# Macaron block on one core: the feed-forward pipeline restaged (first product and count in one slot, second product in one piece) and the row-maximum mask moved

## The chip, the core and the metric

One core of a Trainium2 chip (trn2). The metric is the device time in microseconds of one execution, median of the runs shown. One profiled execution gives the trace that is read below. Engines are called TensorE (PE; its weight loads PEld), VectorE (DVE), ScalarE (ACT), GpSimd (POOL) and SyncE (SP, here only a DMA queue).

## What is computed

Activations `x` of 2 sequences x 1024 tokens x 512. `LN` is a layer normalization without weights.

```
x = x + 0.5 * ffn(LN(x));  x = x + attention(LN(x));  x = x + 0.5 * ffn(LN(x))

ffn(x):       z = x @ ternary(W_syn).T + b_syn            # 512 -> 2048
              thresh = 204th largest of z in the row
              h = where(z >= thresh, relu(z), 0)
              out = h @ ternary(W_out).T + b_out          # 2048 -> 512
              return layernorm(x + out) * gamma + beta
ternary(W):   s = mean|W|;  clip(round(W / s), -1, 1) * s

attention(x): 16 heads of 32, low-rank keys, queries and values; causal softmax; output projection
```

## The kernel before

**Feed-forward.** The 2048 tokens are 16 tiles of 128 rows. Both feed-forwards (f = 0, 1) run the same software pipeline over slots s = -1 to 25. In each slot every engine works through its own list of stages, written out by hand in order; `do(stage, f, s, off)` runs the stage on tile s - off, if that tile exists. Semaphores alone couple the engines. The stages of one tile, with their offsets:

- `stats1`, `normal` (VectorE) and `rstd1` (POOL) at -1: the normalized tile `xn`. `x_turn` (TensorE, four f32 transposes into bank `xP`) at 0, split into an f16 high half `x_hi` (ScalarE) and low half `x_lo` (VectorE).
- `mm1` at 1, in quarters c = 0 to 3 of 512 columns: 8 matmuls of 128x512 for high and low half (line 473) and a bias row (line 478), into `zP`. `evac` (ScalarE, line 709) copies quarters 0 to 2 to `Z` at offset 1, quarter 3 at the head of the next slot (offset 2).
- `count` (ScalarE, line 738) at 2 to 6: five passes of an interpolating search for the threshold, each counting the elements above a trial value in a row of 2048. At the head of a slot `update` (VectorE, lines 1106 to 1127) waits for all counts of the slot before and computes the next trial values of all five tiles; each count waits for it. The updates run in slots 3 (`FIRST_UPD`) to 22 (`LAST_UPD`).
- `S_SEL` = 7: `below` (VectorE, line 1135) masks the tile, `pick` (lines 1141 to 1148) takes the top eight of what is left and the threshold among them and sets a flag per row; `ok_rows` (TensorE, line 519) sums the flags into `xP`; `keep_top` (VectorE) copies the sum to `oki` (line 1206), loads it into a register, branches (`If`, line 1208, an exact search that does not run on this data) and applies the threshold (line 1210). This signals `h_set`.
- `S_OUT` = 8: `h_turn` c (TensorE, line 493) transposes quarter c of the kept tile into one of the two banks of `hP`; from the third on it waits for the low half two quarters back. `h_hi` (ScalarE, line 719) and `h_lo` (VectorE, line 1095) split it; `mm2` c (TensorE, line 506; the last one with a bias row, line 510) multiplies it into `oP`. Quarters 0 and 1 of `mm2` are issued in slot 8 of the tile, 2 and 3 in slot 9, with `h_hi` and `h_lo` of quarter 3.
- `S_FIN` = 9: `residual` (VectorE, lines 1217 to 1221), `rstd2` (POOL), `normal2` (VectorE, line 1229). `final` (POOL, lines 900 to 903) one slot later; it waits for that slot's `below`.

TensorE's list in a slot, in short: `mm1` 0, `h_turn` 0, `x_turn`, `mm2` 2 | `mm1` 1, `h_turn` 1, `mm2` 3 | `mm1` 2, `ok_rows`, `h_turn` 2, `mm2` 0 | `mm1` 3, `h_turn` 3, `mm2` 1. "Full" slots are those with both a first and a second product; the slots ahead of them (the fill) have no second product, the slots behind (the drain) no first product. In the second feed-forward `out_proj` of the attention's second sequence (line 644) stands at the end of slots -1 to 5.

**Attention.** For each sequence and each group of four heads, two units of 512 queries. `core_order` makes one list of events that all engines follow. A "row" event is a score block (line 582) with, on the diagonal, a second matmul that adds the causal mask (line 585); VectorE takes its maximum per query (line 1312). Three banks (`rowP`) take turns. Later "col" events compute the same scores transposed with the maximum folded in (lines 603, 607), ScalarE takes the exponential (line 793), and "mix" events multiply with the values and with ones (line 619).

SP's queue loads the weights, then the attention weights once the last transpose of the first feed-forward is done (line 399).

## Time and profile before

| | |
|---|---|
| median of 3 runs | 1291.21 us (1290.18 to 1293.3) |
| the profiled execution | 1289.8 us, span 1288.0 us |
| mean granted clock of TensorE | 0.939 of 2.4 GHz |
| TensorE busy | 1110.0 us, 86% |
| VectorE busy | 916.6 us, 71% |
| ScalarE busy | 795.9 us, 62% |
| POOL busy | 297.3 us, 23% |
| first feed-forward, attention, second | to 386, to 928, to 1288 us |

Busy shares are averages over stretches with different limits. Where the text says "start to start", it is the distance between the starts of neighbouring instructions on one engine; the printed duration includes a tail that overlaps the next one. A timeline row gives start, duration, engine, line, operation, output and input, and how many instructions are merged (x8); behind it, in brackets, how long the engine was idle ahead of it, and what it waited for.

### The profile page before, as it was taken

What the parts mean: (1) busy time and instruction counts of PE and PEld (TensorE: products, weight loads), DVE (VectorE), ACT (ScalarE), POOL (GpSimd) and SP (SyncE); (2) the same over time, 40 slices, a digit from 0 to 9 for tenths busy, and PEclk for the clock granted to TensorE, in tenths of its full rate; (3) what the DMA queues carried; (4) which work ended last, traced back from release to release, by engine and by line L of the source; (5) the groups of instructions that cost most, each with busy time, mean ns of one, the idle gap of its engine ahead of it and who ended that gap; (6) DMA issues with size and microseconds to landing.
All of it is one profiled execution on the core that took longest, in us unless ns stands there. A gap on an engine that the chain in (4) does not pass through costs nothing.

```text
span 1288.0 us, 17909 instructions
## 1 busy us (share of the span) xinstructions
PE 1110.0 (86%) x6149; PEld 510.9 (40%) x6198; DVE 916.6 (71%) x2010; ACT 795.9 (62%) x1147; POOL 297.3 (23%) x379
## 2 busy tenths in 40 slices
PE   0896999987768789999999799999799799998776
PEld 0342555543334333333344333332244355554333
DVE  5766899889963787875334887782223699999995
ACT  5399888896213536657614356567248998888521
POOL 2100122222252143100220450002100013222224
PEclk9997999998887989999999899999899899999787
DMA  9200000000010122110000311110000000000000
GB/s 370 72 1 1 1 1 2 1 1 1 1 33 21 50 58 50 47 38 2 1 21 8 78 47 46 31 34 2 1 1 1 1 9 10 17 18 18 17 18 33
DMA packets 22284, 37.44 MB, mean 29 GB/s; under 512 B 5398, under 2 KB 7833, under 8 KB 21532
## 3 DMA queue, kind: packets, MB, share of 16 engines
q1 hardware_dynamic: 21404, 34.54, 8.5%
q0 software_dynamic: 768, 1.57, 0.5%
q8 instruction: 50, 0.82, 0.3%
q14 instruction: 62, 0.51, 0.1%
HBM read 19.17 MB, written 4.21 MB: 18 GB/s over the span
## 4 chain that ended last, share of the span: by engine, by line
PE 62%; DVE 20%; issue 7%; ACT 5%; SPq 3%; POOL 1%; DMA 1%; another core or an unknown queue 1%; DVEq 0%; POOLq 0%; ACTq 0%
PE zP L473 13%; PE oP L506 11%; PE xP L619 5%; PE oP L619 5%; PE zP L603 4%; PE zP L544 4%; PE hP L582 3%; PE hP L493 3%; DVE mx L1312 3%; PE hP L644 2%; DVE arena L1095 2%; PE zP L644 2%; DVE arena L1135 2%; ACT arena L738 2%; DVE m L1143 2%
## 5 line engine op out<-in xcount | busy, mean ns | idle before, releaser
L738 ACT ACTIVATE arena<-arena,X 128x2048 int8<-128x2048 f32 x160 | 319.5, 2003 | 4.7 <-DVE X L1127 4.7
L793 ACT ACTIVATE arena<-zP,asc 128x512 f32<-128x512 f32 (+3 forms) x384 | 201.0, 581 | 115.5 <-PE zP L607 84.4
L506 PE MATMUL oP<-T,arena 128*128 128x512 f16 x1024 | 261.2, 402 | 3.0 <-DVE arena L1217 3.0
L473 PE MATMUL zP<-T,arena 128*128 128x512 f16 x1024 | 251.0, 390 | 6.0 <-ACT arena L709 5.1
L1312 DVE TENSOR_REDUCE mx<-hP 128x1 f32<-128x512 f32 (+3 forms) x256 | 135.8, 551 | 36.5 <-PE hP L585 25.0
L719 ACT ACTIVATE arena<-hP,sc 128x512 f16<-128x512 f32 x128 | 88.3, 690 | 106.8 <-PE hP L493 106.8
L473 PEld LDWEIGHTS zP<-T,arena 128*128 128x128 f16 x1024 | 102.3, 100 | 130.3 <-issue 14.6
L506 PEld LDWEIGHTS oP<-T,arena 128*128 128x128 f16 x1024 | 103.4, 102 | 112.1 <-issue 26.3
L709 ACT ACTIVATE arena<-zP,sc 128x512 f32<-128x512 f32 x128 | 87.3, 686 | 81.2 <-PE zP L478 54.8
L603 PE MATMUL zP<-arena 98*128 98x512 f16 (+3 forms) x384 | 110.2, 332 | 2.6 <-DMA arena<-arena 1.7
L1095 DVE SCALAR_TENSOR_TENSOR arena<-hP,sc,arena 128x512 f16<-128x512 f32 x128 | 95.6, 747 | 9.0 <-ACT arena L719 7.9
L1210 DVE SCALAR_TENSOR_TENSOR arena<-arena,sel 128x2048 f32<-128x2048 f32 x32 | 76.7, 2397 | 34.0 <-issue 22.6
L1330 DVE RECIPROCAL arena<-arena 128x128 f32<-128x128 f32 x64 | 57.0, 924 | 61.4 <-ACT arena L806 61.4
L582 PE MATMUL hP<-arena 96*128 96x512 f16 (+3 forms) x256 | 85.2, 349 | 13.3 <-DVE mx L1312 12.9
L900 POOL TENSOR_TENSOR x_sb<-x_sb,bet 128x512 f32<-128x512 f32 x32 | 40.6, 1267 | 222.1 <-DVE arena L1135 222.1
L493 PE MATMUL hP<-identf,arena 128*128 128x128 f32 x512 | 84.2, 290 | 2.7 <-DVE arena L1095 1.4
L619 PE MATMUL oP<-arena 128*32 128x512 f32 (+3 forms) x768 | 81.8, 498 | 3.8 <-ACT arena L806 3.8
L1312 DVE TENSOR_REDUCE mx<-zP 128x1 f32<-128x512 f32 (+3 forms) x128 | 69.8, 546 | 19.9 <-PE zP L585 11.6
L619 PE MATMUL xP<-arena,onesf 128*32 128x512 f32 (+3 forms) x768 | 81.8, 498 | 0.0
L947 POOL TENSOR_TENSOR arena<-arena 128x512 f32<-128x512 f32 x16 | 20.3, 1269 | 255.1 <-DVE arena L1330 255.1
L493 PEld LDWEIGHTS hP<-identf,arena 128*128 128x128 f32 x512 | 68.4, 155 | 25.4 <-issue 4.9
L1135 DVE SCALAR_TENSOR_TENSOR arena<-arena,FIN 128x2048 f32<-128x2048 f32 x32 | 75.0, 2344 | 0.0
(177 smaller groups left out, 1581.6 us busy)
## 6 DMA issues: line engine op xcount, KB each, us to landing
arena<-arena SPq DMA_DIRECT2D x168, 64.0 KB, 2.0
arena<-in_w_synT SPq DMA_DIRECT2D x4, 1024.0 KB, 8.3
arena<-in_w_outT SPq DMA_DIRECT2D x4, 1024.0 KB, 14.7
out_dram<-x_sb SPq DMA_DIRECT2D x16, 256.0 KB, 2.0
x_sb<-in_x SPq DMA_DIRECT2D x3, 1024.0 KB, 14.0
arena<-in_w_o SPq DMA_DIRECT2D x2, 1024.0 KB, 5.0
arena<-arena POOLq DMA_DIRECT2D x24, 64.0 KB, 1.9
arena<-in_b_syn SPq DMA_DIRECT2D x1, 1024.0 KB, 12.1
```

The source lines that it names most:

```text
L473: pe.matmul(zP[:, c * CW:(c + 1) * CW], part[:, g % 2, k, :], T1[:, k, c * CW:(c + 1) * CW], start=(n == 0 and k == 0), stop=False)
L493: mm = pe.transpose(hP[:, c % 2, k * P:(k + 1) * P], Z[:, g % ZR, n0:n0 + P], identf[:, :])
L506: mm = pe.matmul(oP[:, :], part[:, k, :], T2[:, k, :], start=(c == 0 and n == 0 and k == 0), stop=False)
L582: mm = pe.matmul(rowP[bank][:, 0:w], stack[0:3 * HD, 0, h, t * P:(t + 1) * P], stack[0:3 * HD, 1, h, 512 * c:512 * c + w], start=True, sto ...
L603: mm = pe.matmul(colP[m % 3][:, q0:512], stack[0:3 * HD + 2, 1, h, kb * P:(kb + 1) * P], stack[0:3 * HD + 2, 0, h, qc * 512 + q0:(qc + 1) ...
L619: mm = pe.matmul((mixP if kind == "mix_v" else sumP)[h * HD:(h + 1) * HD, q0:512], v, PT[:, m % 2, h, q0:512], start=(kb == 0), stop=last, ...
L719: act.activation(hThi[:, 4 * c:4 * c + 4, :].rearrange("p k t -> p (k t)"), hP[:, c % 2, :], ACT.Copy, scale=SH).then_inc(sm["hT_hi"], 1)
L738: act.activation(junk[:, counted[0] % 2, :], Z[:, g % ZR, :], ACT.Sign, bias=X[:, 2, k:k + 1], accum_out=S[:, k:k + 1]).then_inc(sm["cnt"], 1)
L793: act.activation(PT[:, m // 4 % 2, h, q0:512], colP[m % 3][:, q0:512], ACT.Exp, scale=asc[:, g, 10:11]).then_inc(sm["exp_done"], 1)
L1095: dve.scalar_tensor_tensor(hTlo[:, ks, :].rearrange("p k t -> p (k t)"), hP[:, c % 2, :], SH, hThi[:, ks, :].rearrange("p k t -> p (k t)") ...
L1135: dve.scalar_tensor_tensor(M[:, :], Z[:, g % ZR, :], TF, Z[:, g % ZR, :], ALU.is_le, ALU.mult)\
L1312: dve.tensor_reduce(mx[:, h, t, c:c + 1], rowP[bank][:, 0:w], AX.X, ALU.max)\
```

## The change

All offsets from the count on become one smaller (`S_CNT` = 1: the first count in the slot of the first product; `S_SEL` 6, `S_OUT` 7, `S_FIN` 8), so there is one slot fewer. Quarter 3 is evacuated and its halves are made in their own slot. TensorE's list becomes `h_turn` 0, `mm1` 0, `h_turn` 1, `mm1` 1, `x_turn`, `h_turn` 2, `mm1` 2, `h_turn` 3, `mm1` 3, and then the whole second product `mm2` 0 to 3, with `ok_rows` ahead of quarter 2. VectorE's and ScalarE's lists are put in a new order; `keep_top` is split, so that the flag is read (`read_flag`), the last low half follows, and then the branch. In the attention the mask matmul of the row blocks goes, and VectorE adds a mask tile (`causal`, bf16) while it takes the maximum, in one `tensor_tensor_reduce` whose elementwise result goes to a scratch tile.

```diff
--- before.py
+++ after.py
@@ -25,7 +25,8 @@
 TARGET = TOPK - 4.5
 SSTAR = 2 * TARGET - N
 BIG = 1e30
-S_SEL, S_OUT, S_FIN = 2 + NC, 3 + NC, 4 + NC
+S_CNT = 1
+S_SEL, S_OUT, S_FIN = S_CNT + NC, S_CNT + NC + 1, S_CNT + NC + 2
 ZR = 8
 XR = 11
 XSCALE = 256.0
@@ -218,7 +219,8 @@
         bcols = sb("bcols", [P, 14], F32)
         ident16 = sb("ident16", [P, P], F16)
         identm = sb("identm", [P, P], F16)
-        maskq = sb("maskq", [P, P], F16)
+        causal = sb("causal", [P, 512], BF16)
+        scored = sb("scored", [P, 2, 512], BF16)
         maskk = sb("maskk", [P, P], F16)
         mx = sb("mx", [P, HG, BT, 2], F32)
         mm_ = sb("mm_", [P, HG * 4], F32)
@@ -360,7 +362,7 @@
             if i is not None:
                 stage(f, i, *a)
 
-        FIRST_UPD, LAST_UPD = 3, NT + S_SEL - 1
+        FIRST_UPD, LAST_UPD = S_CNT + 1, NT + S_SEL - 1
 
         def updates(f, s):
 
@@ -578,12 +580,9 @@
                             pe.wait_ge(sm["masks"], 2)
                             pe.wait_ge(sm["a_xT"], (b + 1) * BT)
                         w = min(512, (t + 1) * P - 512 * c)
-                        own = c == t // 4
-                        mm = pe.matmul(rowP[bank][:, 0:w], stack[0:3 * HD, 0, h, t * P:(t + 1) * P],
-                                       stack[0:3 * HD, 1, h, 512 * c:512 * c + w], start=True, stop=not own)
-                        if own:
-                            mm = pe.matmul(rowP[bank][:, w - P:w], identm[:, :], maskq[:, :], start=False, stop=True)
-                        mm.then_inc(sm["row_ps"], 1)
+                        pe.matmul(rowP[bank][:, 0:w], stack[0:3 * HD, 0, h, t * P:(t + 1) * P],
+                                  stack[0:3 * HD, 1, h, 512 * c:512 * c + w], start=True, stop=True)\
+                            .then_inc(sm["row_ps"], 1)
                     elif kind == "turn":
                         pe.wait_ge(sm["m_set"], m + 1)
                         for t in range(4):
@@ -648,16 +647,14 @@
             for f in range(NF):
                 for s in slots:
                     for c in range(4):
+                        do(h_turn, f, s, S_OUT, c)
                         do(mm1, f, s, 1, c)
+                        if c == 1 and (f, s) != (0, 0):
+                            do(x_turn, f, s, 0)
+                    for c in range(4):
                         if c == 2:
                             do(ok_rows, f, s, S_SEL)
-                        do(h_turn, f, s, S_OUT, c)
-                        if c == 0 and (f, s) != (0, 0):
-                            do(x_turn, f, s, 0)
-                        if c < 2:
-                            do(mm2, f, s, S_OUT + 1, c + 2)
-                        else:
-                            do(mm2, f, s, S_OUT, c - 2)
+                        do(mm2, f, s, S_OUT, c)
                     for i in out_tiles(f, s):
                         out_proj(1, i)
                     if f == 0 and s == 0:
@@ -722,7 +719,7 @@
             counted = [0]
 
             def count(f, s, k):
-                i = at(s, 2 + k)
+                i = at(s, S_CNT + k)
                 if i is None:
                     return
                 g = f * NT + i
@@ -815,20 +812,20 @@
             for f in range(NF):
                 for s in slots:
 
-                    do(evac, f, s, 2, 3)
-                    do(h_hi, f, s, S_OUT + 1, 3)
+                    do(h_hi, f, s, S_OUT, 0)
                     do(evac, f, s, 1, 0)
-                    do(h_hi, f, s, S_OUT, 0)
+                    count(f, s, 4)
+                    do(h_hi, f, s, S_OUT, 1)
+                    do(evac, f, s, 1, 1)
                     if (f, s) != (0, 0):
                         do(x_hi, f, s, 0)
-                    count(f, s, 4)
                     count(f, s, 3)
-                    do(evac, f, s, 1, 1)
-                    do(h_hi, f, s, S_OUT, 1)
+                    do(h_hi, f, s, S_OUT, 2)
+                    do(evac, f, s, 1, 2)
+                    do(h_hi, f, s, S_OUT, 3)
+                    do(evac, f, s, 1, 3)
                     count(f, s, 2)
                     count(f, s, 1)
-                    do(evac, f, s, 1, 2)
-                    do(h_hi, f, s, S_OUT, 2)
                     count(f, s, 0)
                 if f == 0:
                     barrier(act, 1)
@@ -843,7 +840,7 @@
         def counts_before(f, s):
 
             per_f = NC * NT
-            return f * per_f + sum(1 for t in range(-1, s) for k in range(NC) if at(t, 2 + k) is not None)
+            return f * per_f + sum(1 for t in range(-1, s) for k in range(NC) if at(t, S_CNT + k) is not None)
 
         @block.gpsimd
         def _(pool):
@@ -866,11 +863,11 @@
             pool.wait_ge(sm["ident_set"], 2)
             link(pool.tensor_copy(ident16[:, :], identf[:, :]))
             link(pool.tensor_scalar(identm[:, :], identf[:, :], MASK, None, ALU.mult))
-            link(pool.memset(maskq[:, :], 0.0))
+            link(pool.memset(causal[:, :], 0.0))
             link(pool.memset(maskk[:, :], 0.0))
 
-            pool.affine_select(out=maskq[:, :], in_=maskq[:, :], compare_op=ALU.is_ge, fill=-MASK, base=0,
-                               pattern=[[-1, P]], channel_multiplier=1).then_inc(sm["masks"], 1)
+            pool.affine_select(out=causal[:, 384:512], in_=causal[:, 384:512], compare_op=ALU.is_ge, fill=-MASK * MASK,
+                               base=0, pattern=[[-1, P]], channel_multiplier=1).then_inc(sm["masks"], 1)
             pool.affine_select(out=maskk[:, :], in_=maskk[:, :], compare_op=ALU.is_ge, fill=-MASK, base=0,
                                pattern=[[1, P]], channel_multiplier=-1).then_inc(sm["masks"], 1)
             link(pool.memset(nhalf[:, :], -0.5))
@@ -1200,13 +1197,19 @@
                     step(dve.tensor_tensor(HIT, HIT, OPEN, ALU.mult))
                     add_found(HIT, BOUND)
 
-            def keep_top(f, i):
+            def read_flag(f, i):
                 g = f * NT + i
                 dve.wait_ge(sm["ok_sum"], g + 1)
                 dve.tensor_copy(oki[:, :], xP[:, 0:1]).then_inc(sm["ok_read"], 1)
+
+            def search_if_open(f, i):
+                g = f * NT + i
                 dve.wait_ge(sm["ok_read"], g + 1)
                 with dve.If(dve.value_load(oki[0:1, 0:1], min_val=0, max_val=P) < P):
                     search_down(Z[:, g % ZR, :])
+
+            def keep_top(f, i):
+                g = f * NT + i
                 dve.scalar_tensor_tensor(Z[:, g % ZR, :], Z[:, g % ZR, :], TH, Z[:, g % ZR, :], ALU.is_ge, ALU.mult)\
                     .then_inc(sm["h_set"], 1)
 
@@ -1309,8 +1312,15 @@
                         h, t, c = e[2:]
                         w = min(512, (t + 1) * P - 512 * c)
                         dve.wait_ge(sm["row_ps"], m + 1)
-                        dve.tensor_reduce(mx[:, h, t, c:c + 1], rowP[bank][:, 0:w], AX.X, ALU.max)\
-                            .then_inc(sm["row_max"], 1)
+                        if c == t // 4:
+                            if m >= 2:
+                                dve.wait_ge(sm["row_max"], m - 1)
+                            dve.tensor_tensor_reduce(scored[:, m % 2, 0:w], rowP[bank][:, 0:w], causal[:, 512 - w:512],
+                                                     1.0, -BIG, ALU.add, ALU.max, mx[:, h, t, c:c + 1])\
+                                .then_inc(sm["row_max"], 1)
+                        else:
+                            dve.tensor_reduce(mx[:, h, t, c:c + 1], rowP[bank][:, 0:w], AX.X, ALU.max)\
+                                .then_inc(sm["row_max"], 1)
                     elif kind == "max":
                         dve.wait_ge(sm["row_max"], n["row"])
                         link(dve.tensor_reduce(mm_[:, :], mx[:, :, 4 * e[2]:4 * e[2] + 4, :], AX.X, ALU.max))
@@ -1360,20 +1370,22 @@
                         ternary(1, s - 2)
                     if FIRST_UPD <= s <= LAST_UPD:
                         update(f, s)
-                    do(h_lo, f, s, S_OUT + 1, 3)
+                    do(h_lo, f, s, S_OUT, 0)
+                    do(residual, f, s, S_FIN)
                     do(below, f, s, S_SEL)
-                    do(h_lo, f, s, S_OUT, 0)
+                    do(h_lo, f, s, S_OUT, 1)
                     if (f, s) != (0, 0):
                         do(x_lo, f, s, 0)
                     if (f, s) == (0, 1):
                         search_start()
                     do(pick, f, s, S_SEL)
-                    do(h_lo, f, s, S_OUT, 1)
-                    do(residual, f, s, S_FIN)
+                    do(h_lo, f, s, S_OUT, 2)
                     if (f, s) != (0, -1):
                         do(stats1, f, s, -1)
+                    do(read_flag, f, s, S_SEL)
+                    do(h_lo, f, s, S_OUT, 3)
+                    do(search_if_open, f, s, S_SEL)
                     do(keep_top, f, s, S_SEL)
-                    do(h_lo, f, s, S_OUT, 2)
                     if (f, s) != (0, -1):
                         do(normal, f, s, -1)
                     if (f, s) == (0, 0):
@@ -1385,6 +1397,7 @@
                     barrier(dve, 1)
                     for i in range(BT):
                         normal_rows(0, i)
+                    dve.wait_ge(sm["masks"], 1)
                     link(dve.memset(mx[:, :, :, :], -BIG))
                     for b in range(2):
                         project(b)
```

## Rows read from the trace of the kernel before

**Rows 1.** Busy time by stretch: us; PE, PEld, DVE, ACT, POOL; clock; DMA.

```profile
189.19:206.44 17.25, 17.20 (x92) 9.29 (x92) 15.72 (x37) 15.12 (x21) 5.36 (x7) 1.00 0.00 1
304.00:319.60 15.60, 11.59 (x56) 5.82 (x55) 14.34 (x33) 9.10 (x12) 4.58 (x5) 0.89 0.00 1
466.00:637.00 171.00, 163.49 (x1348) 58.78 (x1348) 116.41 (x230) 108.77 (x209) 35.28 (x28) 0.98 0.12 32
```

**Rows 2.** The chain of waits in the first attention core, 466 to 637 us.

```profile
by line: PE xP L619 18.4%; PE oP L619 18.3%; PE zP L603 16.4%; PE hP L582 11.9%; DVE mx L1312 9.0%; PE zP L582 5.7%; PE zP L607 3.6%; DVE arena L1330 3.5%; issue 3.2%; ACT arena L793 2.2%; PE hP L585 2.0%; ACT arena L806 1.1%; PE hP L590 1.
```

**Rows 3.** Timeline of TensorE in a steady slot.

```profile
207.68 1.89 PE L473 MATMUL zP<-T,arena 128*128 128x512 f16 x8
...
209.41 0.38 PE L478 MATMUL zP<-brow,bones 128*128 128x512 bf16 x1
...
209.62 0.60 PE L493 MATMUL hP<-identf,arena 128*128 128x128 f32 x4
...
210.06 1.89 PE L506 MATMUL oP<-T,arena 128*128 128x512 f16 x8
```

**Rows 4.** Timeline of VectorE in a steady slot.

```profile
202.84 0.16 DVE L1106 TENSOR_SCALAR X<-S 128x5 f32<-128x5 f32 x1
...
205.21 2.34 DVE L1135 SCALAR_TENSOR_TENSOR arena<-arena,FIN 128x2048 f32<-128x2048 f32 x1
...
207.59 0.75 DVE L1095 SCALAR_TENSOR_TENSOR arena<-hP,sc,arena 128x512 f16<-128x512 f32 x1
...
208.86 0.15 DVE L1141 TENSOR_SCALAR sel<-FIN 128x1 f32<-128x1 f32 x1
...
212.18 0.75 DVE L1095 SCALAR_TENSOR_TENSOR arena<-hP,sc,arena 128x512 f16<-128x512 f32 x1 [0.23 <-ACT arena L719]
212.85 0.74 DVE L1217 SCALAR_TENSOR_TENSOR arena<-oP,sc,arena 128x512 f32<-128x512 f32 x1
...
214.45 0.66 DVE L1069 BATCH_NORM_STATS2 st<-x_sb 128x6 f32<-128x512 f32 x1
...
216.24 2.35 DVE L1210 SCALAR_TENSOR_TENSOR arena<-arena,sel 128x2048 f32<-128x2048 f32 x1 [0.87 <-DVE oki L1206]
```

**Rows 5.** Timeline of ScalarE in a steady slot.

```profile
208.90 2.01 ACT L738 ACTIVATE arena<-arena,X 128x2048 int8<-128x2048 f32 x1
...
210.89 0.69 ACT L709 ACTIVATE arena<-zP,sc 128x512 f32<-128x512 f32 x1
...
212.02 2.01 ACT L738 ACTIVATE arena<-arena,X 128x2048 int8<-128x2048 f32 x1
```

**Rows 6.** Timeline of VectorE: updates of both feed-forwards, the last residual of the first.

```profile
63.18 0.17 DVE L1106 TENSOR_SCALAR X<-S 128x5 f32<-128x5 f32 x1
...
117.37 0.17 DVE L1106 TENSOR_SCALAR X<-S 128x5 f32<-128x5 f32 x1 [0.35 <-ACT arena L738]
...
348.95 0.16 DVE L1106 TENSOR_SCALAR X<-S 128x5 f32<-128x5 f32 x1
...
378.81 0.75 DVE L1217 SCALAR_TENSOR_TENSOR arena<-oP,sc,arena 128x512 f32<-128x512 f32 x1 [3.83 <-PE oP L510]
...
978.95 0.16 DVE L1106 TENSOR_SCALAR X<-S 128x5 f32<-128x5 f32 x1
...
1017.24 0.17 DVE L1106 TENSOR_SCALAR X<-S 128x5 f32<-128x5 f32 x1 [0.31 <-ACT arena L738]
```

**Rows 7.** Timeline of TensorE in a drain slot, first burst behind the flag matmuls.

```profile
312.30 3.17 PE L506 MATMUL oP<-T,arena 128*128 128x512 f16 x8 [0.39 <-DVE arena L1217]
```

**Rows 8.** Timeline: a mask matmul and its successor; a row maximum; an accumulator read.

```profile
546.52 0.22 PE L585 MATMUL zP<-maskq,identm 128*128 128x128 f16 x1
...
546.58 0.38 PE L603 MATMUL zP<-arena 98*128 98x512 f16 x1
...
547.63 0.68 DVE L1312 TENSOR_REDUCE mx<-hP 128x1 f32<-128x512 f32 x1
...
209.19 0.08 DVE L1142 DVE_READ_ACCUMULATOR e<-ranks,sel 128x1 f32 x1
```

## The prediction

> **What bounds the kernel now.** I read the busy time by stretch first. In a steady slot of the feed-forward (17.25 us) TensorE is busy 17.20, VectorE 15.72, ScalarE 15.12, at full clock; in a slot of the drain (15.60 us, no first product left) TensorE has 11.59 and VectorE 14.34; in the first attention core TensorE has 163.5 of 171 us and VectorE 116.4 [rows 1]. The chain of waits inside the core is nearly all TensorE lines, with 9.0% for the row maxima on VectorE [rows 2]. So the change must be priced by stretch. The parts of a steady slot on TensorE, start to start, are: one quarter of a product with its bias row 1.94 us, without it 1.73, four transposes 0.44 [rows 3]. Five groups of transposes, four first-product quarters with bias, four second-product quarters and one bias row (0.21) make 17.1; with the flag matmuls this is the measured 17.25, without a gap.
>
> VectorE's parts, also start to start [rows 4]: a low half of the hidden tile 0.67 (212.18 to 212.85), so the update is 1.71 of the 2.37 from 202.84 to 205.21; `below` 2.38; `x_lo` 0.60 (the rest of 207.59 to 208.86); `pick` 3.1 (208.86 to 212.18, less the 0.23 of waiting printed there); residual with its statistics 1.60. The wait printed in front of `keep_top` begins at 215.37, so `stats1` and the flag's cast fill 0.92 from 214.45 (I split them 0.80 and 0.12), and from the cast to the start of `keep_top` it is 0.99; `keep_top` 2.27, its printed 2.35 less the 0.08 by which neighbours overlap. The slot's remainder to the next update (17.25 after 202.84) is a low half, `normal` and `normal2`, 0.46 each. On ScalarE a count is 1.99 and an evacuation plus a high half 1.13 [rows 5].
>
> **The fill gets shorter.** Each update waits for all counts of the slot before, and each count for its update: 1.83 on the way (1.71, and an estimated 0.12 to the count's start). Before, two evacuations and `x_hi` ran beside the update. After, the count of a tile comes in the slot of its evacuation, and only one evacuation covers the update: with five counts 1.83 + 9.95 + 3 x 0.57 + 0.49 (`x_hi`) + 0.17 (accumulator read; both estimated from their neighbours) = 14.2, where two evacuations less make it 13.1 before. With four counts 11.1 as before, with three 9.0, with two 8.44 (VectorE, which quantizes the second weights then). First feed-forward: the first update, at 63.18, comes one slot earlier, where that slot was 6.7 long without an update: 56.5. Five slots of 8.44, 9.0, 11.1, 14.2, 14.2 give 113.4 for what was at 117.37: 4.0 gained. Second feed-forward: the slots up to 978.95 are set by TensorE (out-projection); two of 14.2 follow, 1007.3 against 1017.24: 9.9 gained [rows 6]. Sum 13.9.
>
> **The full slot gets a VectorE loop.** TensorE's work is the same 17.25. But the order now closes a loop through both engines: update 1.71, low half 0.66, residual 1.60 (moved ahead), `below` 2.38, second low half 0.75 until its signal, then the fourth group of transposes (it needs that bank): 7.14. From there TensorE issues 0.44 + 1.94 + two quarters 3.46 = 5.84 until the flag matmuls, which take 0.40 to VectorE's cast (an estimate, somewhat under the 0.44 of four transposes); 0.99 + 0.07 of dispatch to `keep_top`, 2.27, `normal` and `normal2` 0.92. Sum 17.6 against 17.25. Here I chose that the register load of the `If` runs beside the low half now placed in front of it. Bounds: 17.25 (TensorE alone) and 18.2 (the load waits 0.6 for the low half; no row shows the pair). ScalarE's loop is 17.3 and POOL's three additions still start behind `below`: no cost while they stay under 17.6.
>
> **The drain loses the early second product.** Before, quarters 2 and 3 of the previous tile and quarter 0 stand between the transposes, and VectorE alone sets 15.6. After, quarter 0 waits behind the fourth transposes (7.14 after the update) and the flag matmuls wait behind quarters 0 and 1. With a first product in the slot this is filled; without one TensorE has only 1.75 us of transposes in its first 8 us. In the old drain slot, with 4.0 of 15.6 us idle and a granted clock of 0.89 [rows 1], eight matmuls behind the flag matmuls took 3.17 us [rows 7], against 1.89 in [rows 3]: part of the slot runs at 1.2 and not 2.4 GHz. The Trainium skill has the rule ("TensorE: Matmul & The Clock Gate", "Why this matters for your kernels": keep matmuls dense, an idle stretch drops the clock to half); by it a drain slot is the 17.7 worked out next, and without it the 15.3 of rival B. From rows: at 8.0 start 16 matmuls; all at half speed would be 6.8 us (0.43 each, twice the 0.216 of [rows 3]), all at full 3.46. I take 5.5, nearer to the half, since the burst in [rows 7] was at half for nearly its eight: flag matmuls at 13.5, cast 13.9, `keep_top` 14.95, next update 17.7. Bounds: 15.3 (full speed) and 19.2 (half all through, or the load waits as well).
>
> **From the sixth update to the last** (117.37 to 348.95 before, 231.6 [rows 6]; the same span of the second feed-forward is taken as equal): after, the first full slot 16.9 (no residual), seven of 17.6, two of 17.25 (no further input tile), 1.5 for a start at half clock (bounds 0 and 3), four drain slots of 17.7: 246.9. That is 15.3 lost, twice: 30.6.
>
> **The tail** (last update to the last residual, 348.95 to 378.81: 29.9): flag and `keep_top` 17.3; transposes, high and low half to 19.4; residual of the tile before and second low half to 21.7; fourth transposes, then four quarters in one piece, 7.1 warm plus 2.4 at half clock: residual at 31.8. Bounds 27.4 and 33.5. Twice 1.9: 3.8. What follows (statistics and additions) stays. SP's loads of the attention weights hang on the last transposes, which now lie further ahead of that residual; no cost.
>
> **The attention edit.** The causal mask matmul of the row maxima goes: 256 of 128 columns (4 heads, 8 tiles, 4 groups, 2 sequences), each 0.06 us from its start to the next matmul's [rows 8]: 14.6 us of TensorE. In a stream that is TensorE 95% busy I count three quarters: 11 off. VectorE's maximum becomes an addition of the mask with a maximum. No row has this operation. Lower bound: the 0.68 of a reduce of 512, nothing added. Above it: an accumulator read of 0.08 [rows 8], 256 x 0.08 = 20 us of VectorE; the furthest row is a two-input pass at half rate, taken as 0.3 us more, which would bring VectorE to about 155 of 171. I take 0.08, as with the other accumulating operations. The Trainium skill ("VectorE: DVE Perf Modes", "Two Vector instructions with no wait between them") has an operation that writes out its accumulator as two instructions; by that the read is due, and were it one instruction, the sum would be 3 lower. On the path lie the stretches before the first exponentials and the 9% of [rows 2]: 5 lost. Net 6 gained (bounds: 12 gained, 10 lost). The wait for the own result two operations back is always past. The wider mask costs POOL some 0.3 us early, hidden behind the weight loads.
>
> **Sum.** -13.9 + 30.6 + 3.8 - 6 = +14.5. The profiled execution took 1289.8 us (span 1288.0) and the median is 1291.2, so 1304.3 to 1305.7: 1305.
>
> **Rivals.**
> A (the forecast), chance 0.60: as above, 1305. It decides where TensorE waits for the fourth transposes.
> B, faster, 0.24: TensorE keeps full speed through the drain, because transposes suffice as work, or a second half-speed stretch falls outside the path. Drain slots are then 15.3, the tail 27.4: -13.9 + 2 x (237.3 - 231.6) - 5 - 6 = -13.5, so 1277. For it: one slot fewer in each feed-forward, and the flag's wait covered. Against: [rows 7]. It decides from drain slots under 16.4: 1.3 x 8 less is 10 of the 14.5.
> C, slower still, 0.11: the register load waits for the low half, 0.6 in each of some 30 slots: 1323. [Rows 4] show nothing running beside it.
> D, 0.05: the masked maximum is much dearer than a reduce, and VectorE bounds the core, 10 or more per sequence on top of the forecast's feed-forward: about 1330. Against: old VectorE slack of 55 us per core.
> That the new order does nothing (the loops and the one slot fewer cancel) sits between A and B.
>
> **Numbers.** 1305; range 1277 to 1322, which holds B's figure and nearly C. 0.3% (4 us) is about what a measurement of this kernel can tell from no change. A, C, D leave a little on the near side: faster 0.24, same 0.09, slower 0.67.
>
> **What would show it.** Updates 17.6 us apart in full slots and 17 to 18.5 in the drain; in the drain the fourth transposes released by VectorE's second low half, the first eight matmuls behind them near 3.4 us, the cast waiting for the flag matmuls; a fill slot of 14.2; mask matmuls gone and the core 2 to 4 us shorter. Drain slots near 15.3 with a granted clock near 1.0 would make the forecast wrong, as would an accumulator read that costs 0.2 and more.

## The result, and the profile after

The kernel after takes 1306.9 us (median of 4 runs, 1304.0 to 1308.6), the kernel before 1291.7 (1290.2 to 1293.3): the ratio is 1.0115, with a 95% interval of 1.0091 to 1.0139. The change makes the kernel slower by 15 us, as forecast (1305). The profiled execution of the kernel after is its slowest run, 1308.6 us; against the 1289.8 of the profiled one before that is 18.8 us, and it is these 18.8 us that the traces below divide.

The page of the kernel after: span, busy time, granted clock.

```profile
span 1306.7 us, 17955 instructions
PE 1107.1 (85%) x5942; PEld 494.3 (38%) x5942; DVE 916.1 (70%) x2266; ACT 796.6 (61%) x1147; POOL 301.1 (23%) x379
PEclk9898999997787979999999799999899899998888
```

Busy time by stretch of the kernel after, as in [rows 1]: a steady slot, a drain slot, the first attention core.

```profile
188.49:206.04 17.55, 17.44 (x93) 9.14 (x92) 15.75 (x39) 15.24 (x20) 5.33 (x7) 1.00 0.00 0
309.87:327.05 17.18, 11.48 (x53) 5.95 (x51) 14.35 (x33) 8.58 (x10) 4.55 (x5) 0.80 0.00 0
480.08:649.44 169.36, 161.07 (x1281) 53.38 (x1282) 117.50 (x336) 109.76 (x213) 35.11 (x28) 0.98 0.13 33
```

The work in a drain slot is what it was (TensorE 11.48 us against 11.59, VectorE 14.35 against 14.34), but the slot is 1.6 us longer and the granted clock fell from 0.89 to 0.80. The core is cut here from its first matmul to its first out-projection, 169.4 us; cut alike, the one before took 173.1.

The updates on VectorE and the last residual of the first feed-forward, which answer to [rows 6]:

```profile
59.72 0.17 DVE L1103 TENSOR_SCALAR X<-S 128x5 f32<-128x5 f32 x1
...
116.66 0.17 DVE L1103 TENSOR_SCALAR X<-S 128x5 f32<-128x5 f32 x1 [0.41 <-ACT arena L735]
135.57 0.16 DVE L1103 TENSOR_SCALAR X<-S 128x5 f32<-128x5 f32 x1
...
362.15 0.16 DVE L1103 TENSOR_SCALAR X<-S 128x5 f32<-128x5 f32 x1
...
392.84 0.75 DVE L1220 SCALAR_TENSOR_TENSOR arena<-oP,sc,arena 128x512 f32<-128x512 f32 x1 [6.20 <-PE oP L512]
...
1016.16 0.17 DVE L1103 TENSOR_SCALAR X<-S 128x5 f32<-128x5 f32 x1 [0.36 <-ACT arena L735]
1036.23 0.16 DVE L1103 TENSOR_SCALAR X<-S 128x5 f32<-128x5 f32 x1
```

Cut at these rows, the difference divides as follows (us, after less before; F1 and F2 are the two feed-forwards):

| stretch | forecast | measured |
|---|---|---|
| start and fill, to the sixth update, F1 | -4.0 | -0.7 |
| the same, F2, from its first `x_hi` | -9.9 | -7.5 |
| sixth to last update, F1 | +15.3 | +13.9 |
| the same, F2 | +15.3 | +19.4 |
| tail, last update to last residual, F1 and F2 | +3.8 | +0.8 +0.4 |
| attention, last residual to the next `x_hi` | -6 | -7.7 |
| sum | +14.5 | +18.7 |

### The profile page after: what moved, and what is told of

It is laid out like the page before. It is cut to its first block, busy times and chain, and to the rows that moved or that the text cites. A ratio compares the mean times of both kernels' runs of the same rounds, so it can differ in the third digit from the quotient of the medians.

```text
span 1306.7 us, 17955 instructions
## 1 busy us (share of the span) xinstructions
PE 1107.1 (85%) x5942; PEld 494.3 (38%) x5942; DVE 916.1 (70%) x2266; ACT 796.6 (61%) x1147; POOL 301.1 (23%) x379
## 4 chain that ended last, share of the span: by engine, by line
PE 52%; DVE 26%; issue 12%; ACT 3%; SPq 3%; POOL 1%; DMA 1%; DVEq 1%; POOLq 0%; ACTq 0%
PE oP L508 11%; PE zP L475 7%; PE xP L618 5%; PE oP L618 5%; DVE arena L1132 4%; PE zP L546 4%; PE zP L602 4%; DVE arena L1092 4%; PE hP L583 3%; PE hP L495 3%; PE zP L643 2%; PE hP L643 2%; DVE st L1223 2%; DVE scored L1318 2%; DVE arena L1220 2%
## 5 line engine op out<-in xcount | busy, mean ns | idle before, releaser
L735 ACT ACTIVATE arena<-arena,X 128x2048 int8<-128x2048 f32 x160 | 319.0, 1999 | 14.1 <-DVE X L1124 11.6
L508 PE MATMUL oP<-T,arena 128*128 128x512 f16 x1024 | 249.1, 401 | 0.0
L475 PEld LDWEIGHTS zP<-T,arena 128*128 128x128 f16 x1024 | 102.5, 101 | 116.2 <-issue 14.2
L495 PEld LDWEIGHTS hP<-identf,arena 128*128 128x128 f32 x512 | 61.6, 150 | 104.6 <-DVE arena L1092 78.0
L1318 DVE CUSTOM_DVE_ANT_0 scored<-hP,causal 128x128 bf16<-128x128 f32 (+3 forms) x170 | 80.6, 484 | 19.3 <-PE hP L583 18.1
L1213 DVE SCALAR_TENSOR_TENSOR arena<-arena,sel 128x2048 f32<-128x2048 f32 x32 | 75.2, 2351 | 14.2 <-issue 14.2
L1140 DVE MAX8 m<-arena 128x8 f32<-128x2048 f32 x32 | 73.3, 2290 | 0.0
```

Of the source, the lines that this page charges most:

```text
L475: pe.matmul(zP[:, c * CW:(c + 1) * CW], part[:, g % 2, k, :], T1[:, k, c * CW:(c + 1) * CW], start=(n == 0 and k == 0), stop=False)
L495: mm = pe.transpose(hP[:, c % 2, k * P:(k + 1) * P], Z[:, g % ZR, n0:n0 + P], identf[:, :])
L508: mm = pe.matmul(oP[:, :], part[:, k, :], T2[:, k, :], start=(c == 0 and n == 0 and k == 0), stop=False)
L735: act.activation(junk[:, counted[0] % 2, :], Z[:, g % ZR, :], ACT.Sign, bias=X[:, 2, k:k + 1], accum_out=S[:, k:k + 1]).then_inc(sm["cnt"], 1)
L1318: dve.tensor_tensor_reduce(scored[:, m % 2, 0:w], rowP[bank][:, 0:w], causal[:, 512 - w:512], 1.0, -BIG, ALU.add, ALU.max, mx[:, h, t, c:c ...
```

## The experiments

Times are medians, each with its ratio to the kernel before from the same chip. The first four ran together (before: 1290.0), then e5 to e8 (1289.5), then e9 to e11 (1291.5).

**The attention edit alone, and the feed-forward alone.** `e1_mask_alone` is the kernel before with the mask matmul, `causal`, `scored` and the `tensor_tensor_reduce` of the diff; `e2_feed_alone` is the kernel after with these put back.

> The kernel before with the mask edit alone (the feed-forwards stay as they were). Theory: the two edits are independent, and the trace after shows the attention 7.6 us shorter, 3.7 of it in each core: 1284 us, some 0.994 of before. Rival (the shorter attention of the trace came from the feed-forward's new order around it): no change, 1291 to 1292.

> The kernel after with the mask edit undone: the feed-forward's change alone. Theory: independent edits, so 7.6 us above the kernel after: 1314 to 1315 us, 1.018 of before. Rival (the edits interact): clearly off that sum.

Measured: 1283.9 us (0.9945, 0.9927 to 0.9963) and 1314.6 (1.0187, 1.0157 to 1.0217). The product of the ratios, 1.0131, is within the interval of the whole change: the two parts don't touch. The edit of the attention is a gain; all of the loss is the feed-forward's. What the masked maximum costs shows in VectorE's groups by shape, 400 to 930 us of the kernel after:

```profile
L1322 DVE TENSOR_REDUCE mx<-hP 128x1 f32<-128x512 f32 x86 | 58.9, 685 | 9.5 <-PE hP L583 8.8
...
L1318 DVE CUSTOM_DVE_ANT_0 scored<-hP,causal 128x512 bf16<-128x512 f32 x44 | 29.8, 680 | 5.3 <-PE hP L583 4.9
...
L1318 DVE CUSTOM_DVE_ANT_0 scored<-hP,causal 128x384 bf16<-128x384 f32 x42 | 22.9, 552 | 6.1 <-PE hP L583 5.7
L1318 DVE DVE_READ_ACCUMULATOR2_ANT mx<- 128x1 f32 x256 | 21.1, 82 | 0.0
```

The addition, the second operand and the written result cost nothing: 680 ns against 685 for the plain reduce of 512. There is an accumulator read in a record of its own, 256 times 82 ns, but wherever the next operation is ready (169 of the 256) it starts together with the read:

```profile
545.09 0.69 DVE L1318 CUSTOM_DVE_ANT_0 scored<-hP,causal 128x512 bf16<-128x512 f32 x1
545.70 0.08 DVE L1318 DVE_READ_ACCUMULATOR2_ANT mx<- 128x1 f32 x1
545.70 0.95 DVE L1340 RECIPROCAL arena<-arena 128x128 f32<-128x128 f32 x1
```

From one start to the next it is 0.61 us, the same as from a plain reduce of 512 to the reduce behind it in the kernel before (546.56 to 547.17, the stretch of [rows 8]).

**The residual behind the second low half.** `e3_residual_later` is the kernel after with this on VectorE:

```diff
                     do(h_lo, f, s, S_OUT, 0)
-                    do(residual, f, s, S_FIN)
                     do(below, f, s, S_SEL)
                     do(h_lo, f, s, S_OUT, 1)
+                    do(residual, f, s, S_FIN)
```

> The kernel after; on VectorE the residual stands behind the second low half instead of ahead of below. Theory (a loop from the update over the second low half, the fourth transposes and the flag back to the update): the fourth transposes come 1.6 us earlier. Full slots then fall from 17.55 to TensorE's 17.3 (17.85 to 17.6 in the second feed-forward), drain slots from 17.3 to about 15.7, the tail by 1.6: together some 20 us less, 1287 us. Rival (VectorE's list as a whole sets the slots): its length is the same, no change, 1307 us.

Measured: 1285.4 us (0.9962, 0.9946 to 0.9978). Steady slots are 17.2 us in the first feed-forward and 17.5 in the second, as expected. The loop that it opens is this one in the kernel after, VectorE first (a steady slot), then TensorE:

```profile
201.68 0.16 DVE L1203 CAST oki<-xP 128x1 int32<-128x1 f32 x1 [1.18 <-PE xP L521]
201.75 0.74 DVE L1092 SCALAR_TENSOR_TENSOR arena<-hP,sc,arena 128x512 f16<-128x512 f32 x1
202.70 2.35 DVE L1213 SCALAR_TENSOR_TENSOR arena<-arena,sel 128x2048 f32<-128x2048 f32 x1 [0.21 <-issue]
...
205.88 0.16 DVE L1103 TENSOR_SCALAR X<-S 128x5 f32<-128x5 f32 x1
...
208.25 0.74 DVE L1220 SCALAR_TENSOR_TENSOR arena<-oP,sc,arena 128x512 f32<-128x512 f32 x1
...
212.21 0.75 DVE L1092 SCALAR_TENSOR_TENSOR arena<-hP,sc,arena 128x512 f16<-128x512 f32 x1
```

```profile
201.36 0.28 PE L521 MATMUL xP<-okf,onesf 128*128 128x1 f32 x2
...
213.02 0.66 PE L495 MATMUL hP<-identf,arena 128*128 128x128 f32 x4
```

The fourth transposes start 7.14 after the update. In e3 their row is `212.31 0.60`, with no gap before it. Elsewhere the expectation was less exact: the drain slots average 16.1 us in F1 and 16.3 in F2 (15.7 expected), and the tails are 26.4 and 26.8 where the kernel after has 30.7 and 30.6, so 4.3 and 3.8 us less and not 1.6.

**The clock in the drain.** `e4_warm_drain` is the kernel after with 10 matmuls behind the second and 18 behind the third group of transposes of a drain slot, whose result nobody reads:

```diff
                         do(h_turn, f, s, S_OUT, c)
+                        if c in (1, 2) and at(s, 1) is None and at(s, S_OUT) is not None:
+                            pe.wait_ge(sm["z_evac"], 4 * (f * NT + NT))
+                            for n in range((10, 18)[c - 1]):
+                                pe.matmul(zP[:, 3 * CW:4 * CW], T2[:, 0, 0:P], T2[:, 0, :], start=True, stop=True)
```

> The kernel after with 10 and 18 matmuls of 512 columns without use, into a bank of the first product that is free by then, behind the second and third transposes of each slot of the drain: TensorE is busy while it waits for low halves. Theory (the drain pays for TensorE at half clock): the first two quarters take 3.46 and not 5.3 us, drain slots fall from 17.3 to 15.4, the tail by up to 2: 1286 to 1290 us. Rival (the order alone costs it, the clock does not matter): no change or slower by what the added matmuls delay, 1307 to 1311 us.

Measured: 1293.1 us (1.0026, 1.0012 to 1.0039). TensorE in a drain slot of the kernel after, then of e4:

```profile
330.00 0.66 PE L495 MATMUL hP<-identf,arena 128*128 128x128 f32 x4 [1.72 <-DVE arena L1092]
334.62 1.12 PE L495 MATMUL hP<-identf,arena 128*128 128x128 f32 x4 [3.97 <-DVE arena L1092]
335.53 5.23 PE L508 MATMUL oP<-T,arena 128*128 128x512 f16 x16
340.60 0.28 PE L521 MATMUL xP<-okf,onesf 128*128 128x1 f32 x2
```

```profile
326.79 4.05 PE L654 MATMUL zP<-T 128*128 128x512 f16 x18
330.67 0.60 PE L495 MATMUL hP<-identf,arena 128*128 128x128 f32 x4
331.11 3.62 PE L508 MATMUL oP<-T,arena 128*128 128x512 f16 x16
334.56 0.28 PE L521 MATMUL xP<-okf,onesf 128*128 128x1 f32 x2
```

Behind a gap of 4 us the 16 matmuls take 5.2 us at a granted clock of 0.68 (335.53 to 340.60), behind work that fills it 3.6 at 1.00, which is 2.4 GHz (331.11 to 334.60). Drain slots, which were 17.2 to 18.4, are 15.2 to 15.5. That rule of the Trainium skill ("TensorE: Matmul & The Clock Gate", "Why this matters for your kernels"), keep matmuls dense or the clock halves, agrees with the pair. The tail didn't gain (30.4 us for 30.7): there no `below` stands between the low halves, so the added matmuls were in the way of the fourth transposes, 7.4 us after the first ones instead of 4.5. With that the time is above the theory's 1286 to 1290, and far below the rival's.

**The second product in two pieces again, in the drain alone.** `e5_early_product` puts quarters 0 and 1 behind the third and the fourth transposes there:

```diff
+                    drain = at(s, 1) is None
                     for c in range(4):
                         do(h_turn, f, s, S_OUT, c)
...
+                        if drain and c >= 2:
+                            do(mm2, f, s, S_OUT, c - 2)
...
-                        do(mm2, f, s, S_OUT, c)
+                        if not (drain and c < 2):
+                            do(mm2, f, s, S_OUT, c)
```

> The kernel after, with the second product in two pieces again in the drain slots alone (those without a second product's successor tile ahead): its quarters 0 and 1 are issued right behind the third and the fourth group of transposes, ahead of the flag matmuls as before, but two quarters of 1.73 us no longer stand in one cold burst behind the fourth group; steady slots are untouched. Theory (the drain's price is its order: the flag matmuls wait for two quarters that themselves start cold behind the fourth transposes): quarter 0 runs while the fourth group is awaited, so drain slots come to 15.2 to 15.6 us in place of 17.3, the tail by up to 1 us shorter, full slots stay at 17.55 and 17.86: 1289 to 1292. Rival (the clock alone makes the drain dear, whatever the order): the early quarter runs at half clock too, and drain slots stay within 0.5 us of 17.3: 1303 to 1307.

Measured: 1283.4 us (0.9959, 0.9943 to 0.9975), better than the theory had it. TensorE in its drain slot:

```profile
324.30 1.89 PE L508 MATMUL oP<-T,arena 128*128 128x512 f16 x8
328.18 0.66 PE L495 MATMUL hP<-identf,arena 128*128 128x128 f32 x4 [1.99 <-DVE arena L1096]
328.67 1.89 PE L508 MATMUL oP<-T,arena 128*128 128x512 f16 x8
331.76 0.35 PE L521 MATMUL xP<-okf,onesf 128*128 128x1 f32 x2 [1.21 <-issue]
```

Quarter 0 runs in the middle of the wait for the fourth transposes and leaves 2.0 of the 4.0 us idle, and both quarters run in 1.89 us. The granted clock of this slot is 1.00, where a drain slot of the kernel after had 0.80. Slots are 14.9 to 15.5 us. What the expectation missed is the tail: 25.7 and 25.9, so 5.0 and 4.7 less, where I allowed 1.

**Both, in every slot.** `e6_both` has the edits of e3 and e5 (the expectations from here on call its place "the fourth low half"; it is behind the second, as in e3).

> The residual behind the fourth low half (as in e3_residual_later) and the second product in two pieces in the drain (as in e5_early_product). Theory: the two prices are apart, one in the full slots' loop over the second low half, one in the drain, and add up: full slots 17.2 and 17.5, drain slots 15.0 to 15.4, span 1277 to 1281, time 1278 to 1282. Rival (one loop shows in both places, so that the second repair finds little left): no better than the better of the two alone, 1284 to 1287.

Measured: 1295.3 us (1.0045, 1.0029 to 1.0061), worse than either edit alone; theory and rival both fell. The full slots are e3's (17.2, 17.5), but drain slots are 16.6 to 17.4 and the tails 28.3 and 28.1. TensorE, and VectorE's residual:

```profile
325.94 0.66 PE L495 MATMUL hP<-identf,arena 128*128 128x128 f32 x4 [1.73 <-DVE arena L1096]
329.74 3.57 PE L508 MATMUL oP<-T,arena 128*128 128x512 f16 x8 [3.14 <-DVE arena L1224]
333.11 1.06 PE L495 MATMUL hP<-identf,arena 128*128 128x128 f32 x4
```

```profile
328.85 0.74 DVE L1224 SCALAR_TENSOR_TENSOR arena<-oP,sc,arena 128x512 f32<-128x512 f32 x1
```

The second product writes the bank `oP` that the residual of the tile before reads. e3 had moved that residual back, so the early quarter waited 3.1 us for it, ran at half clock (3.57 for 8), and held up the fourth transposes behind it in TensorE's order: they start 4.2 us after the low half that they need (328.18 to 328.93).

**The turn of the input, one quarter earlier.** `e7_turn_early` is the kernel after with `x_turn` behind quarter 0 of the first product, and `x_hi` ahead of `count` 4:

```diff
-                        if c == 1 and (f, s) != (0, 0):
+                        if c == 0 and (f, s) != (0, 0):
                             do(x_turn, f, s, 0)
...
+                    if (f, s) != (0, 0):
+                        do(x_hi, f, s, 0)
                     count(f, s, 4)
                     do(h_hi, f, s, S_OUT, 1)
                     do(evac, f, s, 1, 1)
-                    if (f, s) != (0, 0):
-                        do(x_hi, f, s, 0)
```

> The kernel after, with the input's transposes of the next tile behind the first quarter of the first product (they stood behind the second), and ScalarE's copy of them ahead of its fourth count. Theory (the start of the first feed-forward was 3.3 us late because the second input tile waits for two quarters of a first product that is still waiting for weights, and a fill slot pays the copy behind the count): first update near 56.5 in place of 59.72, fill slots 13.7 in place of 14.1, all later stretches as in the kernel after: 1301 to 1303. Rival (the start is bound by the loading of the weights, not by that order): first update within 0.5 us of 59.72, and 1305 to 1307.

Measured: 1301.3 us (1.0105, 1.0083 to 1.0128). The five-count fill slots are 13.62, as expected, and the first update comes at 57.27, 2.5 us earlier but not at 56.5. The interval overlaps that of the kernel after (1.0091 to 1.0139), so the gain is read from these places and not from the time. The transposes of the second input tile, in the kernel after and in e7:

```profile
41.37 3.16 PE L475 MATMUL zP<-T,arena 128*128 128x512 f16 x8
44.32 0.63 PE L480 MATMUL zP<-brow,bones 128*128 128x512 bf16 x1
44.75 0.85 PE L460 MATMUL xP<-identf,arena 128*128 128x128 f32 x4
```

```profile
42.08 1.06 PE L460 MATMUL xP<-identf,arena 128*128 128x128 f32 x4
```

`e8_all_three` adds this edit to e6.

> All three repairs on the kernel after: residual behind the fourth low half, second product in two pieces in the drain, input transposes one quarter earlier. Theory (each is a separate price): 33 us less than the kernel after, made of 18 to 20 for the residual's place, 10 to 13 for the drain's order and 3 to 5 for the start, less what the first two share in the drain slots: 1273 to 1277, so faster than the kernel before by some 15 and than the mask edit alone (1284) by some 8. Rival (the fill's gain is taken back by the other places, as a later slot pays what an earlier one saved): 1280 to 1284.

Measured: 1290.2 us (1.0011, 0.9997 to 1.0024): e6 less 5, with e6's drain slots (16.7 to 17.4). Both the theory and the rival missed, for the reason that e6 had shown.

**The residual back in the full slots alone.** `e9_split` is e5 with this; `e10_split_turn` is e9 with e7's edit:

```diff
                     do(h_lo, f, s, S_OUT, 0)
-                    do(residual, f, s, S_FIN)
+                    full = at(s, 1) is not None
+                    if not full:
+                        do(residual, f, s, S_FIN)
                     do(below, f, s, S_SEL)
                     do(h_lo, f, s, S_OUT, 1)
+                    if full:
+                        do(residual, f, s, S_FIN)
```

> The early product of e5_early_product, with the residual behind the fourth low half in the full slots alone; in the drain and the tail it stands ahead of `below`, as in the kernel after. Theory (in e6_both the early quarter waited 3.1 us for the bank that the residual reads, a residual that the same kernel had moved back, and the clock fell in that gap): the two places don't touch, so full slots are 17.2 and 17.5 as in e3_residual_later and drain slots 15.0 and 15.5 as in e5_early_product; 6 us less than e5_early_product (ten slots of 0.34, twice): span 1271 to 1274, time 1274 to 1279. Rival (a shorter full slot takes away the VectorE slack that the drain starts with, or the two repairs share one price): drain slots over 16 again, 1284 or more.

> e9_split with the input transposes one quarter earlier (as in e7_turn_early). Theory: 4 to 5 us less than e9_split, as e7_turn_early gave against the kernel after: span 1267 to 1270, time 1270 to 1275, 15 to 20 under the kernel before and 9 or more under the mask edit alone. Rival (the fill's gain is paid back in the first full slot): no more than 1 us under e9_split.

Measured: 1278.0 us (0.9902, 0.9875 to 0.993) and 1272.8 (0.9856, 0.9832 to 0.988). Full slots 17.2 and 17.5, drain slots 15.0 to 15.6 but for one in each kernel (16.6 in e9, 16.4 in e10). The medians of e9 and e10 differ by 5.2 us, as expected, but the traces show less of it: to the sixth update e10 gains 0.8 us in F1 and 1.0 in F2, since behind the earlier first update of F1 its next two slots are 9.40 and 10.20 us where e9 has 8.45 and 9.18; the rest is not located. What failed in e6 was the shared bank in the drain; in the full slots, where four quarters of the first product stand ahead of the second, the same place of the residual costs nothing.

**The first full slot.** `e11_warm_start` is e10 with 20 matmuls ahead of and 10 behind the flag matmuls in the last fill slot, their result unread:

```diff
+                        if s == S_OUT - 1 and c in (0, 2):
...
+                            for n in range((20, 0, 10)[c]):
+                                pe.matmul(hP[:, 0, :], T1[:, 0, 0:P], T1[:, 0, 0:CW], start=True, stop=True)
```

> e10_split_turn with 30 matmuls of 512 columns, whose results nobody reads, in the last fill slot of each feed-forward (20 ahead of the flag matmuls, 10 behind them, where TensorE stood idle 6 and 4 us). Theory (the first full slot, 18.3 to 20.1 us against the 17.2 to 17.9 of its followers, pays for a start of TensorE at 0.5 granted clock): the first full slot within 0.5 us of the second, 1 to 1.5 us gained in the first feed-forward and 1 to 2.5 in the second, 2 to 4 us under e10_split_turn. Rival (the first full slot is long since ScalarE has two counts more to finish there, or the added matmuls push the flag back): no gain, or up to 2 us lost.

Measured: 1270.2 us (0.9834, 0.9808 to 0.9861). The first full slot goes from 19.1 and 18.3 to 16.2 and 16.6 us, which is 1.5 less than the second and not within 0.5 of it. Busy time around the sixth update, e10 and then e11:

```profile
112.90:117.00 4.10, 3.63 (x11) 1.92 (x12) 3.00 (x17) 2.33 (x3) 0.00 (x0) 0.50 0.00 0
```

```profile
112.80:117.00 4.20, 4.04 (x25) 2.46 (x24) 3.10 (x17) 3.44 (x6) 0.00 (x0) 1.00 0.00 0
```

Eleven matmuls at a granted clock of 0.50 against 25, unread ones among them, at 1.00. From the sixth update to the last it saves 2.9 us in F1, more than the 1 to 1.5 expected, and 1.9 in F2; the medians differ by 2.6, though the runs of the two overlap by 2. It is the fastest kernel here, 1.7% under the kernel before.

## Why the prediction was right, and where its terms were off

The direction and the amount were right, and so was the cause of the loss: from the sixth update to the last 30.6 us were forecast as lost and 33.3 were. Part of the near hit is luck: the terms miss by +5.7 (fill), +2.7, -2.6 (tail) and -1.7 (attention), 4.2 together. And these are terms of the profiled runs, 18.8 us apart; the medians are 15.2 apart, since the profiled run lies 1.9 below the median before and 1.7 above it after.

**The loop of the full slot: right in each step.** 7.14 from the update to the fourth transposes (205.88 to 213.02), forecast 7.14 (its five parts add to 7.10; the rest is the transposes' start behind the low half); 6.2 from there to the cast, forecast 6.24; from the cast to `keep_top` 1.02, forecast 1.06; slot 17.55, forecast 17.6. The choice that the register load runs beside the low half (rival C) holds: with the low half in between, cast to `keep_top` is no longer than the 0.99 of before. e3 shows the loop: open it, and the slot of the first feed-forward is 17.2, TensorE's own length.

In the second feed-forward slots are 17.86, which the prediction left out. The row of `keep_top` there:

```profile
1104.59 2.35 DVE L1213 SCALAR_TENSOR_TENSOR arena<-arena,sel 128x2048 f32<-128x2048 f32 x1 [0.52 <-issue]
```

The wait for issue behind the `If` is 0.52 us where the first feed-forward has 0.21. The kernel before has the same difference (cast to `keep_top` 1.30 against 1.00), but TensorE bounded its slot and hid it; the new loop runs through it, 0.3 us in each slot. Why the branch costs more there stays open. It is also why e3's slot is still 17.52 there: the fourth transposes no longer wait, but the first ones of the next slot do, for `keep_top`. In e3, VectorE and then TensorE:

```profile
1109.81 2.35 DVE L1213 SCALAR_TENSOR_TENSOR arena<-arena,sel 128x2048 f32<-128x2048 f32 x1 [0.52 <-issue]
```

```profile
1111.74 0.38 PE L512 MATMUL oP<-brow,bones 128*128 128x512 bf16 x1
1112.21 0.66 PE L495 MATMUL hP<-identf,arena 128*128 128x128 f32 x4
```

`keep_top` ends at 1112.16, and TensorE, free at 1111.95, starts at 1112.21; in the first feed-forward this gap is missing. Over the nine full slots behind the first the branch takes 2.8 of the 5.5 us by which the second feed-forward lost more than the first; the first full slot (1.2) and the drain (1.3) make the rest of it but 0.3.

**The drain: right, in place and price.** The burst starts 8.04 after the update (forecast 8.0), its 16 matmuls take 5.1 (5.5), the next update comes after 17.2 to 17.5, in F2 up to 18.35 (17.7). e4 shows that the half clock is the price (17.3 to 15.4 us), e5 that the new order brings the half clock about. Rival B, full clock all through the drain, is what e4 and e5 had to make: the transposes alone did not do it, one quarter of the product in the middle of the gap did.

**The start of the first full slot: undersized.** 18.9 and 20.1 us for 18.4. e11 gives the price of the cold start as 2.9 and 1.8 (against e10), where 1.5 was taken (bounds 0 and 3). That slot also varies by itself: in kernels whose order up to it is that of the kernel after it took 18.3 to 19.0 us in F1 and 18.4 to 20.1 in F2, which stays open.

**The fill: the step that failed.** The five-count slot is 14.1, forecast 14.2. But the first update was forecast one slot earlier, at 56.5, and it came at 59.72. I let the second tile's transposes start as before (41.44), though the diff puts them behind a second quarter of the first product: 44.75. The other kernels divide the 3.2 us. With the transposes behind the second quarter, and this quarter at half clock (2.9 to 3.4 us for its 8 matmuls, in the kernel after, e2, e3, e4 and e6), the first update comes at 59.7 to 60.7; with the same order and the quarter at full clock (1.89 us, e5 and e9) at 58.3 and 58.5; with the transposes ahead of it (e7, e8, e10, e11) at 56.4 to 57.3. So the place costs some 1.6 us, and the half clock, which some of the traces show on that quarter and others don't, some 1.3.

In F2 the first update does come one slot earlier, but the slots before the five-count ones are 12.3, 13.6 and 11.6 where I kept the 11.6 of before, set by TensorE. This is another step, since e7 has the same 12.3 and 13.6. TensorE does keep its 11.6 (the input's transposes start at 953.50, 965.13 and 976.77), but three of the counts now stand behind the evacuation of the last quarter, so a further count moves the update back, by 0.6 and 2.0 us.

**The tail: oversized.** It was 30.7 us for 31.8. The four quarters took 7.95 (384.47 to 392.42) where I had 7.1 and 2.4 more for the half clock.

**The attention: right, a little small.** VectorE's read is there but overlaps, so rival D (a dear maximum) falls, and the 20 us of reads cost nothing on the path. The Trainium skill ("VectorE: DVE Perf Modes", "Two Vector instructions with no wait between them") has the read as a second instruction; the trace agrees, 256 records. The share that TensorE gives back was right, the amount that leaves it was not: in the first core, cut alike, it is busy 161.1 us for 166.1, so 5.0 less, and the core is 3.7 shorter (3.6 in the second), about the three quarters forecast. The forecast took 7.3 us per sequence; 107 of the 128 mask matmuls lie in the core by the trace. The chain of waits in the core, for [rows 2]:

```profile
by line: PE oP L618 19.0%; PE xP L618 18.6%; PE zP L602 16.9%; PE hP L583 12.2%; issue 8.2%; PE zP L583 5.9%; DVE scored L1318 4.1%; PE zP L606 3.8%; DVE arena L1340 2.7%; ACT arena L790 2.2%; DVE mx L1322 1.7%; ACT arena L803 1.1%; PE hP L
```

The maxima are 5.8% of it (9.0% before), where 5 us of loss on the path were forecast. Issue has grown from 3.2 to 8.2%, and by the mask edit (e1 has 8.1%, e2 3.2%), though TensorE's idle time in the core only went from 7.0 to 8.3 us; what this share consists of stays open.

**Open.** The attention, the same code in all kernels with the mask edit, took 541.5 to 545.8 us from profile to profile; differences below 4 us between kernels are read from the slots for that reason. Single drain slots of 16.4 to 16.8 in e9 to e11 are not explained.

## What to carry to other kernels

One slot fewer in a pipeline is worth what the fill and the drain are worth, and is paid in every full slot if the stages that moved closer close a loop through two engines: add up that loop before the engines' busy times. When an order is shortened, cut the list by phase (fill, full, drain), since the best place of one step can differ between them; and where two repairs are combined, look for the buffer that one of them frees and the other wants (here the bank of the second product), and for whatever is queued behind the wait. In a phase in which TensorE has slack, spread its work over the wait instead of gathering it behind.

## What the runs showed of the hardware

- A `tensor_tensor_reduce` out of PSUM with a written bf16 result takes what a plain reduce takes (680 against 685 ns at 512, 552 at 384), and its accumulator read, 82 ns, overlaps the next operation.
- Behind 4 us without work TensorE ran 16 matmuls in 5.2 us at a granted clock of 0.68; in e5, behind gaps of 1.4 and 2.0 us with 8 matmuls between them, 8 took 1.89 us, at 1.00.
- Behind the branch on a register VectorE waits 0.20 to 0.22 us for issue in most slots of the first feed-forward (0.56 in the last two) and 0.52 to 0.55 in the second (1.2 in the first slot of each), with the same code and the same outcome.
